# Perceiver layer on one core: the experts' stage with its products split in three and its outputs kept by channel, and queries split likewise

## Reference

```python
x = x + xattn(layernorm(x), ctx)                 # 16 heads of 32 channels
x = x + mamba(layernorm(x))                      # ... y * silu(res) @ w_out
# third part, on layernorm(x), which is called x here:
xc = causal_conv(x, dw_kernel, 3 taps) + dw_bias
x1 = x + silu(xc @ pw_w.T + pw_b)
logits = x1 @ router_w.T + router_b              # 8 experts, the best 2 are taken
rw = softmax over the best two, 0 for the other six
ye = silu(x1 @ expert_w[e].T + expert_b[e])      # all 8 experts
combined = sum over e of rw[e] * ye[e]
h = norm_w * rmsnorm(x1 + combined @ out_w.T + out_b)
out = x + h + gelu(h @ ff_down.T + ff_down_b) @ ff_up.T + ff_up_b
```

## Time and profile before

| | before |
|---|---|
| median of 3 runs | 2108.8 us (2108.29 to 2114.44) |
| the profiled execution's own time | 2113.07 us |
| its span | 2111.2 us |
| TensorE busy, share of the span | 1991.5 us, 94% |
| VectorE busy | 1437.0 us, 68% |
| ScalarE busy | 884.8 us, 42% |
| GpSimd busy | 1177.6 us, 56% |
| mean granted TensorE clock | 0.978 of 2.4 GHz |

### The profile page before, as it was taken

How to read it: one execution, slowest core, us unless ns; L and a number is a source line. 1 busy time by engine, 2 the same in 40 slices (tenths; PEclk the granted TensorE clock), 3 DMA queues, 4 the chain that set the end, 5 groups by cost and what they waited for, 6 DMA issues and landing times. The chain is left out here.

```text
span 2111.2 us, 41942 instructions
## 1 busy us (share of the span) xinstructions
PE 1991.5 (94%) x15559; PEld 1420.4 (67%) x15559; DVE 1437.0 (68%) x1472; ACT 884.8 (42%) x1267; POOL 1177.6 (56%) x843
## 2 busy tenths in 40 slices
PE   6989999999999999999998879899999999899999
PEld 3767777777777777777764458555555554378874
DVE  5126766666666666666667737399999994846655
ACT  1124444444444444444434544466676651133310
POOL 3126666666666666666657621189989992322200
PEclk9999999999999999999998889999999999999999
DMA  4545465555555555555553220310040003012101
GB/s 175 153 141 168 152 179 162 173 171 163 175 156 174 161 171 169 167 169 164 166 168 106 76 62 1 81 42 1 1 120 1 1 25 101 0 46 70 55 0 41
DMA packets 180470, 227.38 MB, mean 108 GB/s; under 512 B 21456, under 2 KB 111824, under 8 KB 174128
## 3 DMA queue, kind: packets, MB, share of 16 engines
q1 hardware_dynamic: 180272, 224.68, 34.9%
HBM read 151.07 MB, written 73.53 MB: 106 GB/s over the span
## 5 line engine op out<-in xcount | busy, mean ns | idle before, releaser
L452 POOL TENSOR_TENSOR a_half<-a_pt 128x1024 f32<-128x1024 f32 x128 | 306.9, 2397 | 348.9 <-ACT a_pt L519 339.3
L519 ACT ACTIVATE a_pt<-a_shift 128x2048 f32<-128x2048 f32 x128 | 245.2, 1916 | 482.3 <-PE a_o L834 371.8
L633 DVE TENSOR_TENSOR a_shift<-a_s,a_neg_rows 128x2048 f32<-128x2048 f32 x113 | 259.0, 2292 | 170.2 <-ACT a_neg_rows L536 170.2
L620 DVE TENSOR_REDUCE a_top<-a_s 128x128 f32<-128x2048 f32 x113 | 258.7, 2290 | 47.4 <-PE a_s L787 47.3
L746 PE MATMUL a_pj<-l_x_hi,l_w_hi 128*128 128x512 f32 x448 | 198.7, 443 | 0.0
L1221 POOL TENSOR_TENSOR s_even_drive<-s_du,l_rows 128x512 f32<-128x512 f32 x128 | 162.7, 1272 | 63.1 <-DMA s_c_row<-bc_scratch 60.4
L443 POOL TENSOR_TENSOR l_x_lo<-a_raw,l_x_hi 128x512 fp32r<-128x512 f32 x120 | 152.9, 1274 | 73.8 <-ACT l_x_hi L506 73.8
L746 PE MATMUL a_pj<-l_w_hi,l_x_hi 128*128 128x512 f32 x448 | 185.5, 414 | 0.0
L1229 POOL TENSOR_TENSOR s_odd_seen<-s_odd_state,s_c_row 128x512 f32<-128x512 f32 x128 | 162.3, 1268 | 34.0 <-DVE s_odd_state L1360 14.5
L1421 PEld LDWEIGHTS s_ps<-s_diag,s_du_t 128*128 128x128 f32 x1024 | 135.9, 194 | 61.9 <-issue 61.9
L748 PE MATMUL a_pj<-l_x_lo,l_w_hi 128*128 128x512 f32 x448 | 177.4, 396 | 0.0
(11 more groups left out here) (235 smaller groups left out, 3981.1 us busy)
## 6 DMA issues: line engine op xcount, KB each, us to landing
kv_scratch<-a_k_new SPq DMA_DIRECT2D x128, 256.0 KB, 2.5
kv_scratch<-a_v_new SPq DMA_DIRECT2D x128, 256.0 KB, 3.7
a_stack<-kv_scratch SPq DMA_DIRECT2D x512, 64.0 KB, 2.3
a_v<-kv_scratch SPq DMA_DIRECT2D x32, 1024.0 KB, 6.2
a_raw<-in_ctx SPq DMA_DIRECT2D x120, 256.0 KB, 3.4
a_q_stack<-q_scratch SPq DMA_DIRECT2D x128, 64.0 KB, 2.1
s_c_row<-bc_scratch SPq DMA_DIRECT2D x32, 256.0 KB, 5.9
e_ew_raw<-in_ew SPq DMA_DIRECT2D x8, 1024.0 KB, 4.8
```

Source lines behind the costliest of these rows:

```text
L452: nc.gpsimd.tensor_tensor(half[:], w[:, 0:2], w[:, 2:4], ALU.add).then_inc(halved, 1)
L519: nc.scalar.activation(pt_head(g, p), shift[:].rearrange("p (i n) -> p i n", n=BANK), ACT.Exp).then_inc(exped, 1)
L620: dve.tensor_reduce(top[:], s_ps[:].rearrange("p i n -> p (i n)").rearrange("p (k q) -> p q k", q=L), AX.X, ALU.max).then_inc(blocked, 1)
L633: dve.tensor_tensor(shift[:].rearrange("p (k q) -> p k q", q=L), s_ps[:].rearrange("p i n -> p (i n)").rearrange("p (k q) -> p k q", q=L), ...
```

## The change

Queries: the product is split (hi by ScalarE, lo by GpSimd for the weights and by VectorE for x), ScalarE writes the normalised batch, VectorE only prepares `rstd` and `shift_by`, and the wait for the stores of q_scratch moves into the next block. Attention's last batch: `shift_by` is made with `tensor_scalar` in place of `scalar_tensor_tensor`, and `statistics` goes behind `shift_half`. Mixer input: the seven small tables are loaded ahead of `at`.

Experts' stage: batch 0 of the mixer's output product stays float32, batches 1 to 7 are split, with `u` split batch by batch in two buffers; the convolution's first tap goes to ScalarE; `pw`, `ow` are split; the router is done in two groups; the expert tiles are 128 channels by 512 tokens, so the bias goes into ScalarE's silu, and the route weights are transposed, stored to DRAM and read back spread over all partitions (`late`), by which VectorE multiplies and then adds; no transposes of `comb`; sums of squares by a product with one column of `ones`, their roots on 4 columns, spread again over the columns by a product with a diagonal; h is turned back as transposes into `tp` and added by VectorE.

```diff
 def queries(...):
-            for b in range(B):
+            def normalise(b):
+                act.wait_ge(scaled, b + 1)
+                ...
+                nc.scalar.activation(xn[:, b % 2], xt[:, b, :], ACT.Identity, bias=shift_by[:, b:b + 1],
+                                     scale=rstd[:, b:b + 1]).then_inc(normed, 1)
...
-            sp.wait_ge(stored, 32 * KC)
 def attention(...):
-                dve.scalar_tensor_tensor(out=shift_by[:, j:j + 1], in0=mv[:, j, 0:1], scalar=-1.0, in1=rstd[:, j:j + 1],
-                                         op0=ALU.mult, op1=ALU.mult).then_inc(ln.scaled, 1)
+                dve.tensor_scalar(shift_by[:, j:j + 1], mv[:, j, 0:1], rstd[:, j:j + 1], -1.0, ALU.mult, ALU.mult)\
+                   .then_inc(ln.scaled, 1)
...
 def mixer_in(...):
+            for dst, src in ((bi, b_in), (wc, w_conv), (bc, b_conv), (wx, w_x)) + to_load:
+                sp.dma_start(dst[:], src).then_inc(w_in_s, 16)
+            sp.wait_ge(ln.a_stored, 16 * KC * B)
             sp.dma_start(at[:], a_scratch[J]).then_inc(a_in, 16)
...
 def experts(...):
         # GpSimd
+            for b in (1, 2, 3):
+                rest_of_output(b)
+            for n in range(2):
+                rest_of_pointwise(2 * n)
+                rest_of_pointwise(2 * n + 1)
+                rest_of_output(4 + n)
+            for half in range(2):
+                rest_of_expert(0, half)
+                rest_of_output(6 + half)
+            for n in range(NT):
+                rest_of_convolved(n)
         # ScalarE
+            round_output(1)
+            for c in range(DT):
+                nc.scalar.copy(wo_hi[:, c], rows[:, c]).then_inc(w_hi_out, 1)
+            round_output(2)
+            for b in range(B):
+                normalise(b)
+                if 1 <= b and b + 2 < B:
+                    round_output(b + 2)
+                if b >= 1:
+                    take_turned(b - 1)
+                if b in (1, 2):
+                    round_pointwise(2 * b - 2)
+                    round_pointwise(2 * b - 1)
+                if b == 3:
+                    round_expert(0)
+                if b == 4:
+                    start_convolution(0)
+                if b == 5:
+                    start_convolution(1)
+                    start_convolution(2)
+                    round_convolved(0)
+                if b == 6:
+                    start_convolution(3)
+                    round_convolved(1)
+                    round_convolved(2)
+            round_convolved(3)
+            take_turned(B - 1)
+            for n in range(KC, NT):
+                start_convolution(n)
+            round_convolved(4)
+            for n in range(KC - 1):
+                silu_pointwise(n)
+                round_convolved(KC + 1 + n)
         # VectorE
+            for c in range(DT):
+                dve.wait_ge(w_hi_out, c + 1)
+                dve.tensor_tensor(wo_lo[:, c], rows[:, c], wo_hi[:, c].bitcast(F32), ALU.subtract).then_inc(wo_lo_out, 1)
...
+            def weigh_expert(e, n):
+                i = NT * e + n
+                k, cols = tile_of(n)
+                if n == 0:
+                    dve.wait_ge(route_in[e % 2], 16 * (e // 2 + 1))
+                dve.wait_ge(act_out, i + 1)
+                dve.tensor_tensor(act_e[:, i % 4], act_e[:, i % 4], late[:, e % 2, cols], ALU.mult).then_inc(weighed, 1)
+                dve.wait_ge(weighed, 2 * i + 1)
+                dve.tensor_tensor(h_t[:, k, cols], h_t[:, k, cols], act_e[:, i % 4], ALU.add).then_inc(weighed, 1)
...
         # TensorE
+            pointwise(0)
+            pointwise(1)
+            turn_normalised(B - 1)
+            pointwise(2)
+            pointwise(3)
+            route_group(0)
+            for n in range(KC, NT):
+                pointwise(n)
+            route_group(1)
...
-            for b in range(B):
-                turn(comb[:, b, :], b, B + b, comb_out, (E - 1) * B + b + 1)
```

More of the change, by code:

```diff
@@ L1663, in _, with statistics @@
-            finish_norm(B - 1)
-            dve.wait_ge(copied, B)
+                    if j:
+                        dve.wait_ge(taps, 2 * n + j)
+                    dve.scalar_tensor_tensor(out=c, in0=xf_t[:, k, BG * (n // KC):BG * (n // KC) + BG, j:j + L],
+                                             scalar=dw[:, k, j:j + 1], in1=c, op0=ALU.mult, op1=ALU.add).then_inc(taps, 1)
+            def statistics(b):
+                dve.wait_ge(made, b + 1)
+                dve.tensor_tensor(xres[:, b, :], xres[:, b, :], ps[:, b % 4, :], ALU.add).then_inc(chain, 1)
+                dve.wait_ge(chain, added_no(b))
+                dve.bn_stats(stats[:, b, :], xres[:, b, :]).then_inc(chain, 1)
+                dve.wait_ge(chain, stats_no(b))
+                dve.bn_aggr(mv[:, b, :], stats[:, b, :]).then_inc(chain, 1)
+                dve.wait_ge(chain, mean_no(b))
+                dve.tensor_scalar(rstd[:, b:b + 1], mv[:, b, 1:2], EPS, None, ALU.add).then_inc(chain, 1)
@@ L1726, in _ @@
[L1726 to L1729 removed]
+            dve.tensor_tensor(route[:], route[:], second[:], ALU.add).then_inc(lg_out, 1)
+            dve.wait_ge(turned, B + 1)
+            dve.wait_ge(copied, B)
+            dve.tensor_copy(route_t[:], tp[0:B * E, 0, 0:L]).then_inc(lg_out, 1)
@@ L1841, in _, with route_group @@
-            squares(1)
+            def route_group(g):
+                pe.wait_ge(x1_out, KC * (g + 1))
+                for b in range(BG * g, BG * g + BG):
+                    for k in range(KC):
+                        mm = pe.matmul(ps[:, 4, b * E:(b + 1) * E], x1_t[:, k, batch(b)], rw[:, k, :],
+                                       start=(k == 0), stop=(k == KC - 1))
+                    if g:
+                        mm.then_inc(made, 1)
+            pointwise(0)
+            pointwise(1)
```

743 lines of the change are left out of this document (449 added, 294 removed).

## The result

| | before | after |
|---|---|---|
| median, 20 runs each | 2111.68 us (2106.49 to 2117.71) | 2103.72 us (2099.16 to 2109.62) |
| after / before | | 0.9966, 95% interval 0.9956 to 0.9975 |
| profiled execution, its span | 2113.07, 2111.2 us | 2103.7, 2101.9 us |
| granted clock | 0.978 | 0.972 |

By the ratio the kernel is 7.2 us faster (5.3 to 9.3; the two medians of the table differ by 8.0), half of the 14 us forecast. The 20 runs of the kernel before have a median 2.9 us above the three on which the forecast stood.

A forecast was written before the change was run, and what follows sets the result against it. TensorE was taken as busy nearly throughout, with loose places in the queries and attention's last batch. Terms -6 - 5 + 0 + 8 + 1 - 12 = -14 took 2108.8 to 2094.8, taken as 2095 us; forecast 2088 to 2101, range 2083 to 2109.

The forecast's parts named there:

- Queries: Queries' stage: split products and normalising moved from VectorE to ScalarE start the next stage earlier; -6 us, bounds -8 and -3.
- The mixer input: Mixer input: tables first free ScalarE earlier, but `at` comes later and batch 7's path stays; 0, bounds -2 and +3.
- The list of pauses: Experts' stage to its first expert product: TensorE pauses behind batch 0, ahead of batch 7 and ahead of the router's first half.
- From `ow` to the end: Tail behind the last expert product: `ow` follows at once, 55 to 58 us to the end; -12 us, bounds -15 and -9.
- Experts: +1 us: Experts: the first weighing waits some 20 us for spread weights, 0 to 2 us lost; +1 us, bounds 0 and +5.
- the forecast's own signs of being wrong: Subtractions at 0.69 beside busy GpSimd, TensorE idle within the experts, or spread weights landing over 8 us after issue.
- rival 4: Experts: VectorE becomes the bound, alternating with GpSimd at 3.1 us a tile, 24 us more, 2119 us; chance 0.1.
- The front, "+8": Experts' stage to its first expert product: waits for rests and sums, and slow clocks; +8 us, bounds 0 and +14.
- Attention, "-5": Attention's last batch: faster `shift_by` and statistics behind the shift let the shift start sooner; -5 us, bounds -8 and 0.
- The first (no lock): Experts' stage front: VectorE and GpSimd don't hold each other for `tensor_tensor`; front 0 instead of +8, 2087 us; chance 0.15.
- rival 2: Queries and attention: the small `tensor_scalar` waits for GpSimd too; last batch +1, queries -4, 2103 us; chance 0.1.
- The third: Experts' stage front: queues pile up further; front +14 to +20, 2101 to 2107 us, largely no change; chance 0.15.

The follow-up runs named there:

- Experiment 4: Changed kernel with the spread weights stored by expert, so each 512 KB read is 128 packets of 4 KB instead of 1024 of 512 B; single run 2108.1 us.
- repeat: The changed kernel measured and profiled once more, on the same chip as three kernels beside it; median 2105.39 us, 0.9972 of the kernel before.
- experiment 8: Changed kernel with GpSimd's first rest of u held back until VectorE has made all eight rests of wo; single run 2108.2 us.
- experiment 1: Changed kernel's stages ahead of the experts' stage with that stage as before: 0.9946 of the kernel before; the other way round: 1.0034.
- mended kernel: Changed kernel with the edits of experiments 2 to 7, batch 1 of the output product in float32 and GpSimd's rests reordered; median 2074.3 us, 0.9821 of the kernel before.
- experiment 5: Changed kernel with ScalarE's rounding of u for batch b+2 ahead of its normalising pass of batch b; 0.9957 of the kernel before.
- experiment 6: Changed kernel with the fourth convolved tile rounded ahead of batch 7's normalising pass in ScalarE's list; 0.9954 of the kernel before.
- experiment 2: Changed kernel with the router's first half behind the pointwise tiles instead of between them; 0.9939 of the kernel before.
- Experiment 10: Measured the changed kernel again (0.9972 of the kernel before) and one with the waits found so far mended (0.9821, median 2074.3 us).

## Why the prediction was off

**The steps that held.** Queries -6.0. VectorE no longer writes `xn`; its small instructions take 0.15 to 0.21 us beside GpSimd. The mixer input: 0 for the stretch; TensorE waited 2.2 us for `at` (2.5), but its fifth tile, which was to keep its place within 0.3 us, came 1.5 us later. The list of pauses, step by step, in us from the start of the experts' stage: batch 1 ends at 17.8 (forecast 18), batches then come every 6.3 (6.2), batch 7 ends at 61.6 (61), `pw` starts at 69.5 (70), its four tiles end at 82.5 (83), the router's first half starts at 91.9 (92) and ends at 98.9 (98.5). Ahead of batch 7 there were pauses of 0.8 and 2.8 us where some 5 had been named. That the steps agree to 1 us is in part luck with the clock: in the eight profiles whose lists are those of the changed kernel up to there, the first pause is always 3.3 us, but batch 1 ends anywhere from 16.1 to 19.0 and `pw` starts from 67.9 to 70.8. From `ow` to the end 57.8, and 58.6 to 58.9 in most other runs (58.1). `ow` followed the last expert without a gap.

**The step that failed most: "Experts: +1 us".** It measured +4.8 us. Its mechanism stood there, four banks and a weighing that has to come in time; the sum was mis-sized. I allowed 20 us for transpose, store and read from the row of another spread transfer (5.9 us, 256 KB), and 0 to 2 us lost. The weights were there at 23.5 us, the read alone taking 8.7, and the stretch took 4.8 us longer: 3.05 us of pause and 1.8 us of slow clock behind it. The read was issued at 14.8 us, so it makes 2.8 of the 3.5 us by which the weights were late against 20. Experiment 4 shows that the read was the cause: with an eighth of the packets, laid in one piece, it lands in 3.7 us and the stretch is back at 176.5. This read had pieces of 512 B, 4 KB apart, which I did not look at. The row that I had used, pieces of 2 KB, was no clean price either: 256 KB took 5.9 us there, longer than 512 KB in pieces of 4 KB take here, and what else held it isn't shown. Two of the forecast's own signs of being wrong came with this step: the read landed more than 8 us after its issue, and TensorE stood idle within the experts, though by the read and not by rival 4.

**The front, "+8", measured +9.8 and up to +12.7.** Up to the end of the router's first half every step is right to 1 us in this profile. The rest is the clock: the four tiles behind the router took 13.2 us, not 12.6, and the second half 4.0 us in this run but 6.45 in its repeat, where TensorE had fallen to half clock again behind the 1.5 us pause. Timeline of the repeat:

```profile
1862.36 6.45 PE L2040 MATMUL e_ps<-e_rw,e_x1T 128*128 128x8 f32 x32 [1.50 <-DVE e_x1T L1874]
```

I had priced it at full clock, 3.2 us. The lock that the forecast named for the first pause is shown by experiment 8; it is worth 1.4 us of pause there, and up to 2.9 us more where a slow clock follows.

**The experts' stage as a whole.** The forecast had it at -3 us (+8 + 1 - 12). It measured +2.4 us in the pair of profiles and +7.2 (5.1 to 9.5) by the runs of experiment 1, while everything ahead of it gave -11.4 against a forecast of -11. So the whole miss lies in this stage: by the profiles first in the experts, then in the front. What the runs miss beyond the pair fits the front, which was shortest in the pair's profile; that is argued, not shown.

**Attention, "-5", by its mechanism right,** 1.25 us a head on average over the six heads, 7.5 us in all where I had 7.9 "by the trace", and small against the spread of the same instructions: over eleven profiles with the changed list attention took 1173.1 to 1180.0 us against 1184.8 and 1185.1 with the old one, so -5 to -12.

**The rivals.** The first (no lock) fell by experiment 8, and the Trainium skill's rule (SBUF — State Buffer, Who interferes with whom), that a `tensor_tensor` with two inputs in SBUF waits for GpSimd's reads, agrees with 8.80 against 4.91 us. The second (the small `tensor_scalar` waits too) fell by 0.21 us in every batch, in attention's last batch each time within a GpSimd instruction of 2.36 us; so the +1 that the forecast had worked out for that case did not come. The fourth (VectorE bounds the experts) fell: its two instructions average 0.84 and 0.89 us, 1.7 a tile against TensorE's 2.72. The third, queues that pile up in the front, describes what happened in part, +9.8 to +12.7 instead of +14 to +20, but not through queues: through the clock. Two small slips of the forecast's sums change nothing: 0.74 for faster leaves 0.04 of rival 2's 0.1, which isn't "most" of it, and the range's ends stand 1 and 2 us outside the figures that they are said to come from (2084 and 2107).

**What I did not ask.** The forecast took the pauses of the experts' stage as the price of splitting. For the most part they were the price of the order of four lists. TensorE's busy time in that stretch fell by 8 us, to 91.0, and in the mended kernel it is 83.5 of 91.1 us; where I looked, the instruction that TensorE waited for had its data early and stood behind another that had not (experiments 5, 6), or TensorE had other work that was nearer (2). Experiment 10 shows what that was worth: 26 to 29 us in that stretch. Not separated is how much of it each of its edits gives; alone, experiments 2, 5 and 6 gave 2.5 to 7 there, and one edit, batch 1 in float32, splits less instead of changing an order.

## What to carry to other kernels

When products get shorter, go through each wait of the matmul engine and ask what stands ahead of the needed instruction in its engine's list and was itself waiting: mending the lists, together with the read, gained 31 us here, the change itself 7. Price a pause of TensorE at its length and a range for the half clock behind it: 0 to 2.9 us here for pauses of 2.0 to 8.7 us ahead of large products, and not by their length. Keep small-column products in short pieces between large ones. Lay data that is read back spread over all partitions so that each partition's piece lies in one stretch and goes as one packet.

## What the runs showed of the hardware

- A read of 512 KB spread over 128 partitions lands after 8.7 us in 1024 packets of 512 B whose pieces stand 4 KB apart (7.8 with no other read beside it) and after 3.7 us in 128 packets of 4 KB.
- VectorE's 128x512 subtraction of two SBUF operands, paced by ScalarE's roundings, goes at 0.61 us each alone and 1.10 beside GpSimd's two subtractions.
- 16 products of 8 columns in float32 (32 records) take 3.8 to 4.0 us near full clock and 6.3 to 7.0 at or mostly at half clock, and 32 in a row took 9.5 us though TensorE came to them from full work. In the mended kernel pieces of 4 such products between large ones left the clock at 1.00 (first row below). 16 products with one column between large ones took 3.85 us at a clock of 0.93, but the large products right behind them ran at 0.50 (second and third row, changed kernel).

```profile
1814.20:1823.20 9.00, 8.32 (x49) 1.00 0.00 0
```

```profile
2057.70:2061.40 3.70, 3.70 (x34) 0.93 0.02 4
2061.40:2063.40 2.00, 2.00 (x6) 0.50 0.00 0
```

- The same pause of TensorE can be followed by half clock or not: behind 3.3 us ahead of batch 1 the next 24 records took 5.7 us in three profiles, 7.3 in four and 8.4 to 8.6 in three.
